# An image laid out as channel and pixel-row pair on 96 partitions, its channel sums in two products, and the third fold moved

## The chip, the core and the metric

The kernel runs on one core of one Trainium2 chip. The metric is device time in microseconds: the median of several executions of the whole kernel.

A core has TensorE (PE), which multiplies matrices into PSUM banks; VectorE (DVE), ScalarE (ACT) and GpSimd (POOL) for elementwise work; and SyncE (SP), which here issues most DMAs. Each engine works through its own queue in order, and engines wait for each other by semaphores.

## What is computed

Inputs are 64 images of 12 channels of 224 x 224 pixels, and 32 text tokens of 192 numbers for each. Three parts follow on each other:

```python
# tokens: 16 x 16 pixels summed, then a weighted sum of the channels
pooled = x.reshape(B, 12, 14, 16, 14, 16).sum(axis=(3, 5))
h = einsum('bcij,ce->bije', pooled, channel_weights).reshape(B, 196, 192)
h = concatenate([h, txt], axis=1)                    # 228 tokens an image
# attention: 12 heads of 16, rotary, causal, with a sink column
h = h + attn(layernorm(h))
# a mixture of 8 experts, top 2, each with a capacity
h = h + moe(layernorm(h))
```

The change touches the first two lines alone, and the time at which some of their work is done.

## The kernel before

**Two passes.** The first pass runs over the 64 images, the second over the 8 experts with tiles of 456 rows. The second is not touched.

**The first pass is a pipeline of five stages.** In each step, image p is pooled (`p`), p-1 gets its queries, keys and values (`a`), p-2 its score maxima (`m`), p-3 its softmax and attention (`t`), and p-4 its projection, routing and scatter (`z`). There are 68 steps; the first six and the last four are written out, the others are a loop over two steps each. Within a step each engine has an order written by hand: `step_tensor` (L1048), `step_scalar` (L1100), `step_vector` (L1144), `pass1_gpsimd` (L1234) and `pass1_sync` (L1210). A stage in brackets below names the batch on which an item works.

**The way of an image.** `load_image` (L404) brings it in one DMA, on 112 partitions: 4 channels x 14 patch rows x 2 halves of a patch row. The free dimension holds three groups (`g`, 4 channels each) of 8 pixel rows x 224. There are two buffers (`xin`), and a load waits until the image two before is pooled (`x_pooled`); SP comes to it one step ahead, so that it is issued as soon as that pooling ends. Then, for each group:

1. `fold_image` (L682, POOL) adds the second 4 pixel rows onto the first 4: one instruction (L686) of 896 elements a partition.
2. `pool_image` (L497, DVE) sums 4 rows x 16 pixels: one reduction (L502) of 896 elements to 14.
3. `spread_patches` (L689, POOL) multiplies the 14 sums with a mask `patch` into 196 columns (L694), so that a partition has its sums only at its own patch row.

`sum_channels` (L837, PE) then makes, for each of two halves of the 196 tokens, three matmuls (L844) that add over the 112 partitions of each group with the channel weights `chan`. Each fp32 matmul is two records in the trace. `copy_h` (ACT) takes the sums out of bank 6.

**The order around the change.** On TensorE the end of a step is T0 T1 T2 (a, L906), `turn_shift` (m, L939), `make_v` (a, L871), `turn_y` (t, L995), T3 T4 T5 (a), `sum_channels` (p, L844), `turn_yn` (t, L1003); the score products S (`score_t`) and C (`score`) open the next step. `turn_shift` waits for `shift_made` and for `routed`; `turn_yn` for `y_normed`.

On DVE it is the maxima 3 to 6 with two pool_images and two `rotate`s (L533, L535) between, pool_image 2, maxima 7 and 8 (L571), `make_shift` (m, L578), `assign` (z, L664 to L679, of which L675 signals `routed`), place_k 1 (a, L559), `split_shift` (m, L586), `weigh` (z), place_k 3, `normalize` (t, L593 and L598, signals `y_normed`), place_k 5.

`make_shift` takes a maximum of two SBUF tensors:

```python
nc.vector.tensor_tensor(shift[:, :, 0:2 * HEADS]..., top[:, :, :]...,
                        sink_tok[:, :]..., ALU.max).then_inc(shift_made, 1)
```

The operands of nearly all other frequent DVE instructions of the pass lie in PSUM, at least one of the two.

On POOL it is inverse_std (a), fold 0, inverse_std (z), fold 1, add_rotation 0 (a, L719), fold 2, add_rotation 1, low_parts 0 and 1 (a, the remainders, two instructions L726 each, the last of them behind ACT's `high_parts` 1), the three spreads, and four scatters (L1284) of an older batch.

Of the kernel before, what the change touches and what calls it, by code (L numbers as in the profile page):

```python
# [21 lines left out]
GRP = 4  # L22
NG = CH // GRP
XP = GRP * SIDE * 2
XF = HALF * IMG
D = 192
# [22 lines left out]
def constants(tokens):  # L49
# [29 lines left out]
    rows = np.arange(XP)  # L79
# [10 lines left out]
        "patch": ((rows[:, None] // 2) % SIDE == np.arange(SIDE)[None]).astype(f),  # L90
# [5 lines left out]
               "before", "patch", "filler"]  # L96
# [28 lines left out]
def build(nc, x, txt, chan_w, norm_scale, norm_bias, w_attn, b_attn, w_proj, b_proj, sinks,  # L125
# [17 lines left out]
    with ctx:  # L143
# [23 lines left out]
        patch = sb("patch", [XP, SIDE])  # L167
        filler = sb("filler", [TT, 2, 2, RW], u32)
        chan = sb("chan", [XP, NG, D])
# [12 lines left out]

        arena = sb("arena", [128, 2 * NG * XF])
        xin = [arena[0:XP, NG * XF * i:NG * XF * (i + 1)].rearrange("p (g f) -> p g f", g=NG) for i in range(2)]
        pooled = [sb(f"pooled{i}", [XP, NG, SIDE]) for i in range(2)]
        spread = sb("spread", [XP, NG, SIDE * SIDE])
# [68 lines left out]
        def view(parts, a, b):  # L255
            nonlocal taken
            taken += a * b
            assert taken <= 2 * NG * XF
            return arena[0:parts, taken - a * b:taken].rearrange("p (a b) -> p a b", a=a)
# [41 lines left out]
        x_spread = sem("x_spread")  # L301
# [52 lines left out]
        N_SMALL = 25  # L354


        def setup_sync(sp):
            for dst, src in (
                (cos[:, :, :], const["cos"]), (sin[:, :, :], const["sin"]), (ident[:, :], const["ident"]),
                (split[:, :], const["split"]), (small[:, :], const["small"]),  # L360
                (patch[:, :], const["patch"]), (filler[:, :, :, :], const["filler"]),
                (scale_col[:, :], norm_scale.rearrange("(c p) -> p c", p=C)),
                (bias_col[:, :], norm_bias.rearrange("(c p) -> p c", p=C)),
                (w_qkv[0:C, :, :], w_attn.rearrange("(c p) n -> p c n", p=C)),
                (b_row, b_attn.rearrange("(a n) -> a n", a=1)),
                (rez[:, :], rezero.rearrange("(a n) -> a n", a=1).to_broadcast([C1, 1])),
                (sink_tok[:, :], sinks.rearrange("(a n) -> a n", a=1).to_broadcast([TT, HEADS])),
                (gate[:, :, :], gate_t.rearrange("(c p) n -> p c n", p=C)),
            ):
# [30 lines left out]
        x_img = x.rearrange("b (g c) (q r) w -> b (c q) g (r w)", g=NG, r=HALF)  # L400
# [281 lines left out]
        def fold_image(pool, at, g):  # L682

            pool.wait_ge(x_loaded[at.par], 16 * (at.half + 1))
            mid = XF // 2
            nc.gpsimd.tensor_tensor(xin[at.par][:, g, 0:mid], xin[at.par][:, g, 0:mid], xin[at.par][:, g, mid:XF],  # L686
                                    ALU.add).then_inc(x_folded, 1)

        def spread_patches(pool, at):  # L689

            wait(pool, h_summed, at.b)
            for g in range(NG):
                pool.wait_ge(x_pooled, NG * at.b + g + 1)
                ins = nc.gpsimd.tensor_tensor(spread[:, g, :].rearrange("p (i j) -> p i j", j=SIDE),  # L694
                                              pooled[at.par][:, g, :].unsqueeze(1).to_broadcast([XP, SIDE, SIDE]),
                                              patch[:, :].unsqueeze(2).to_broadcast([XP, SIDE, SIDE]), ALU.mult)
            ins.then_inc(x_spread, 1)
# [139 lines left out]
        def sum_channels(pe, at):  # L837

            n = at.b + 1
            pe.wait_ge(x_spread, n)  # L840
            wait(pe, v_ready, at.b)
            for t, (lo, hi) in enumerate(((0, TT), (TT, SIDE * SIDE))):
                for g in range(NG):
                    ins = nc.tensor.matmul(bank[6][0:hi - lo, D * t:D * (t + 1)], spread[:, g, lo:hi], chan[:, g, :],  # L844
                                           start=(g == 0), stop=(g == NG - 1))
# [298 lines left out]
        def step_vector(dve, p, a, m, t, z):  # L1144
# [25 lines left out]
            if p:  # L1170
                pool_image(dve, p, 2)
# [5 lines left out]
            if a:  # L1177
                place_k(dve, a, 1)
            if m:
# [54 lines left out]
        def pass1_gpsimd(pool):  # L1234
            def one(half, par, known=None, fill=None):
# [12 lines left out]
                if p:  # L1248
                    fold_image(pool, p, 2)
                if a:  # L1250
# [3 lines left out]
                if p:  # L1254
                    spread_patches(pool, p)
# [446 lines left out]
```

## Time and profile before

| | |
|---|---|
| median of 3 runs | 2946.89 us (2943.04 to 2951.11) |
| the profiled execution | 2948.84 us, of which the span in the trace is 2947.0 |
| PE, matmuls | 2785.7 us busy, 95% of the span |
| DVE | 2049.3 us, 70% |
| POOL | 2023.1 us, 69% |
| ACT | 1693.0 us, 57% |
| first pass | to about 1740 us |

A row of a timeline reads: start in us, duration in us, engine, line of the kernel, operation, output <- inputs, then output and input shapes (partitions x elements; for a matmul stationary rows * columns first), the number of merged records, and in brackets the engine's idle time before it and who ended it. Busy shares are averages; what a change is worth is read from what is late at the place it touches.

### The profile page before, as it was taken

The numbers are of one execution on the slowest core, as the hardware profiler recorded it, in microseconds if no ns is written. First come the engines' busy times: TensorE is split into PE (matmuls) and PEld (weight loads), VectorE is DVE, ScalarE is ACT, GpSimd is POOL, SyncE is SP. The second block draws the span as 40 slices with busy tenths as digits, with TensorE's granted clock in tenths as the row PEclk, the third lists the DMA queues.
The fourth block names the chain that finished last, engine by engine and source line by source line (L and its number), as shares of the span: only waits on it lengthen the run. The fifth ranks groups of instructions, "written<-read, shape, count | busy, mean of one in ns | idle before, by whom it ended". The sixth has DMA issues, their size and how long they took to land. (4 is left out here: it accounts for less than half of the span.)

```text
span 2947.0 us, 65980 instructions
## 1 busy us (share of the span) xinstructions
PE 2785.7 (95%) x21712; PEld 2512.3 (85%) x21712; DVE 2049.3 (70%) x5657; ACT 1693.0 (57%) x4074; POOL 2023.1 (69%) x2070
## 2 busy tenths in 40 slices
PE   2899999999999999999999976999999999999998
PEld 0788888888888888888888865999999989998997
DVE  3477777777777777777777745777676767676766
ACT  0365666666666666656666644656565656555655
POOL 2478888888888888888888833666555656565665
PEclk9899999999999999999999987999999999999999
DMA  6444555543444444334444113333333333323242
GB/s 177 145 163 162 172 177 182 160 117 106 109 116 121 121 121 117 110 104 115 121 121 121 54 43 68 50 60 56 63 50 61 56 61 54 66 45 66 44 70 43
DMA packets 206006, 292.47 MB, mean 99 GB/s; under 512 B 95670, under 2 KB 167675, under 8 KB 205874
## 3 DMA queue, kind: packets, MB, share of 16 engines
q1 hardware_dynamic: 82994, 243.82, 28.3%
q0 software_dynamic: 122880, 47.00, 11.3%
q8 instruction: 69, 1.13, 0.2%
q14 instruction: 63, 0.52, 0.1%
HBM read 201.73 MB, written 93.90 MB: 100 GB/s over the span
## 5 line engine op out<-in xcount | busy, mean ns | idle before, releaser
L1493 POOL DMA_INDIRECT out<-arena,who x320 | 596.0, 1862 | 292.1 <-DVE who L1372 179.7
L686 POOL TENSOR_TENSOR arena<-arena 112x896 f32<-112x896 f32 x192 | 403.0, 2100 | 44.0 <-DMA arena<-in_x 44.0
L571 DVE TENSOR_REDUCE top<-bank 114x2 f32<-114x456 f32 (+1 forms) x576 | 352.7, 622 | 87.3 <-PE bank L930 71.1
L1466 PE MATMUL bank<-w_dn,hid 128*114 128x192 f32 x3840 | 401.9, 264 | 0.0
L1466 PEld LDWEIGHTS bank<-w_dn,hid 128*114 128x114 f32 x3840 | 390.3, 180 | 0.0
L1439 ACT ACTIVATE arena<-bank 128x456 f32<-128x456 f32 x320 | 176.3, 551 | 341.8 <-PE bank L1430 331.8
L1284 POOL DMA_INDIRECT moe_rows<-row,slot x256 | 294.5, 1150 | 77.3 <-issue 73.7
L548 ACT ACTIVATE pieces<-bank 64x456 fp32r<-64x456 f32 x384 | 209.4, 545 | 147.1 <-PE bank L906 144.8
L1443 DVE TENSOR_TENSOR arena<-bank,arena 128x456 f32<-128x456 f32 x320 | 201.5, 630 | 94.9 <-ACT arena L1439 82.4
L726 POOL TENSOR_TENSOR qk<-rot_c,qk 114x384 fp32r<-114x384 f32 x256 | 253.9, 1014 | 18.3 <-ACT qk L747 18.3
L1426 PE MATMUL bank<-pieces 128*128 128x456 f32 x640 | 240.2, 375 | 22.5 <-DVE arena L1443 15.5
L805 ACT ACTIVATE prob<-bank 115x456 f32<-115x456 f32 x384 | 208.0, 542 | 80.7 <-PE bank L956 80.0
L1455 DVE TENSOR_TENSOR hid<-arena,hid 128x456 fp32r<-128x456 f32 x320 | 201.6, 630 | 52.3 <-ACT hid L1450 34.3
L1430 PE MATMUL bank<-pieces 128*128 128x456 f32 x640 | 237.8, 372 | 0.0
L1450 ACT ACTIVATE hid<-arena 128x456 fp32r<-128x456 f32 x320 | 187.0, 584 | 87.9 <-DVE arena L1443 86.7
L1429 PE MATMUL bank<-pieces 128*128 128x456 f32 x640 | 237.1, 371 | 0.0
L1427 PE MATMUL bank<-pieces 128*128 128x456 f32 x640 | 236.2, 369 | 0.6 <-issue 0.4
L1428 PE MATMUL bank<-pieces 128*128 128x456 f32 x640 | 236.7, 370 | 0.0
L502 DVE TENSOR_REDUCE pooled<-arena 112x14 f32<-112x896 f32 x192 | 206.7, 1076 | 26.4 <-POOL arena L686 26.4
L1483 POOL TENSOR_TENSOR rms<-rms,minus_half 114x4 f32<-114x4 f32 x82 | 85.4, 1041 | 190.3 <-DVE rms L1364 190.3
L906 PE MATMUL bank<-ident_r,qk 114*128 114x114 f32 x1536 | 202.1, 282 | 10.6 <-POOL qk L726 10.6
L906 PEld LDWEIGHTS bank<-ident_r,qk 114*128 114x128 f32 x1536 | 186.5, 196 | 23.0 <-POOL qk L726 22.9
(171 smaller groups left out, 7211.4 us busy)
## 6 DMA issues: line engine op xcount, KB each, us to landing
arena<-in_x SPq DMA_DIRECT2D x64, 2352.0 KB, 11.9
arena<-moe_rows SPq DMA_DIRECT2D x82, 363.4 KB
moe_rows<-filler SPq DMA_DIRECT2D x20, 1453.5 KB
out<-h SPq DMA_DIRECT2D x64, 171.0 KB
out<-arena,who POOLq DMA_INDIRECT x320, 5.0
arena<-in_w_t SPq DMA_DIRECT2D x9, 512.0 KB, 6.8
arena<-in_w_t SPq DMA_DIRECT2D x18, 256.0 KB, 7.7
moe_rows<-row,slot POOLq DMA_INDIRECT x256, 7.1
```

The source lines that it names most:

```text
L571: nc.vector.tensor_reduce(dst, src, AX.X, ALU.max).then_inc(maxed[k], 1)
L686: nc.gpsimd.tensor_tensor(xin[at.par][:, g, 0:mid], xin[at.par][:, g, 0:mid], xin[at.par][:, g, mid:XF], ALU.add).then_inc(x_folded, 1)
L726: ins = nc.gpsimd.tensor_tensor(lo, of, first.bitcast(fp32), ALU.subtract)
L906: ins = nc.tensor.matmul(dst[:, TT * (2 * pair + half):TT * (2 * pair + half + 1)], src, ident_r[0:TT, 0:TT], start=True, stop=True)
L1284: nc.gpsimd.indirect_dma_start(out=moe_rows[0:SLOTS, :], out_offset=bass.IndirectOffsetOnAxis(ap=slot[at.par][:, 2 * t + k:2 * t + k + 1], ...
L1426: nc.tensor.matmul(dst, hi[:, 0, col], za_hi[:, :], start=True, stop=False)
L1427: nc.tensor.matmul(dst, hi[:, 0, col], za_lo[:, :], start=False, stop=False)
L1428: nc.tensor.matmul(dst, lo[:, 0, col], za_hi[:, :], start=False, stop=False)
L1429: nc.tensor.matmul(dst, hi[:, 1, col], zb[:, :], start=False, stop=False)
L1430: ins = nc.tensor.matmul(dst, lo[:, 1, col], zb[:, :], start=False, stop=True)
L1466: ins = nc.tensor.matmul(dst, hid2[:, j, h_part, at], w_dn2[e_par][:, j, w_part, :], start=(j == 0 and s % 2 == 0 and part == 0), stop=(j ...
L1493: nc.gpsimd.indirect_dma_start(out=out[:, :], out_offset=bass.IndirectOffsetOnAxis(ap=who[par][:, s:s + 1], axis=0), in_=ys[par][:, s, :], ...
```

## The change

**Layout.** A partition now holds one of 12 channels and one of 8 pairs of pixel rows within a patch row: 12 x 8 = 96 partitions. The free dimension is 14 patch rows of 2 x 224 pixels. An image comes by 8 DMAs, one for each pair of pixel rows, 12 partitions each.

**Folds and pools.** A fold adds the second pixel row of each pair onto the first, and a pool sums 16 pixels. They are done in three bands of patch rows, 5, 5 and 4 of the 14, where three groups of channels were.

**Channel sums.** A partition now has all 196 patch sums of its channel and row pair, so `pooled` goes straight into the matmul, with the channel weights repeated for the 8 row pairs: two matmuls instead of six. `spread_patches`, its mask and its semaphore are gone; `sum_channels` waits for `x_pooled`.

**Order.** On POOL fold 2 moves from behind add_rotation 0 to behind low_parts 1, where the spreads were. On DVE pool_image 2 moves from before maxima 7 and 8 to behind place_k 1, before split_shift.

```diff
-GRP = 4
-NG = CH // GRP
-XP = GRP * SIDE * 2
-XF = HALF * IMG
+XP = CH * HALF
+XF = 2 * IMG
+BANDS = ((0, 5), (5, 10), (10, SIDE))
+NG = len(BANDS)
...
-        chan = sb("chan", [XP, NG, D])
+        chan = sb("chan", [XP, D])
...
-        arena = sb("arena", [128, 2 * NG * XF])
-        pooled = [sb(f"pooled{i}", [XP, NG, SIDE]) for i in range(2)]
-        spread = sb("spread", [XP, NG, SIDE * SIDE])
+        arena = sb("arena", [128, 2 * SIDE * XF])
+        pooled = [sb(f"pooled{i}", [XP, SIDE * SIDE]) for i in range(2)]
...
-            for g in range(NG):
-                sp.dma_start(chan[:, g, :], chan_w[GRP * g:GRP * (g + 1), :].unsqueeze(1)
-                             .to_broadcast([GRP, SIDE * 2, D])).then_inc(loaded, 16)
+            sp.dma_start(chan[:, :], chan_w.unsqueeze(0).to_broadcast([HALF, CH, D])).then_inc(loaded, 16)
...
-        x_img = x.rearrange("b (g c) (q r) w -> b (c q) g (r w)", g=NG, r=HALF)
+        x_img = x.rearrange("b c (i r s) w -> b r c i (s w)", r=HALF, s=2)
...
-            sp.dma_start(xin[at.par][:, :, :], x_img[at.b, :, :, :]).then_inc(x_loaded[at.par], 16)
+            for r in range(HALF):
+                sp.dma_start(xin[at.par][CH * r:CH * (r + 1), :, :], x_img[at.b, r, :, :, :]).then_inc(x_loaded[at.par], 16)
...
             if g == 0:
-                wait(dve, x_spread, at.b - 1)
+                wait(dve, h_summed, at.b - 1)
             dve.wait_ge(x_folded, NG * at.b + g + 1)
+            lo, hi = BANDS[g]
             ins = nc.vector.tensor_reduce(
-                pooled[at.par][:, g, :],
-                xin[at.par][:, g, 0:XF // 2].rearrange("p (r j c) -> p j r c", r=HALF // 2, c=PATCH), AX.XY, ALU.add)
+                pooled[at.par][:, SIDE * lo:SIDE * hi],
+                xin[at.par][:, lo:hi, 0:IMG].rearrange("p i (j c) -> p i j c", c=PATCH), AX.X, ALU.add)
...
-            pool.wait_ge(x_loaded[at.par], 16 * (at.half + 1))
-            mid = XF // 2
-            nc.gpsimd.tensor_tensor(xin[at.par][:, g, 0:mid], xin[at.par][:, g, 0:mid], xin[at.par][:, g, mid:XF],
+            pool.wait_ge(x_loaded[at.par], 16 * HALF * (at.half + 1))
+            lo, hi = BANDS[g]
+            nc.gpsimd.tensor_tensor(xin[at.par][:, lo:hi, 0:IMG], xin[at.par][:, lo:hi, 0:IMG], xin[at.par][:, lo:hi, IMG:XF],
                                     ALU.add).then_inc(x_folded, 1)
-
-        def spread_patches(pool, at):
...
-            pe.wait_ge(x_spread, n)
+            pe.wait_ge(x_pooled, NG * n)
...
-                for g in range(NG):
-                    ins = nc.tensor.matmul(bank[6][0:hi - lo, D * t:D * (t + 1)], spread[:, g, lo:hi], chan[:, g, :],
-                                           start=(g == 0), stop=(g == NG - 1))
+                ins = nc.tensor.matmul(bank[6][0:hi - lo, D * t:D * (t + 1)], pooled[at.par][:, lo:hi], chan[:, :],
+                                       start=True, stop=True)
...
             maxima("6")
-            if p:
-                pool_image(dve, p, 2)
             maxima("7 8")
...
                 place_k(dve, a, 1)
+            if p:
+                pool_image(dve, p, 2)
             if m:
                 split_shift(dve, m)
...
                     add_rotation(pool, a, 0)
-                if p:
-                    fold_image(pool, p, 2)
-                if a:
                     add_rotation(pool, a, 1)
                     low_parts(pool, a, 0)
                     low_parts(pool, a, 1)
                 if p:
-                    spread_patches(pool, p)
+                    fold_image(pool, p, 2)
```

## Rows read from the trace of the kernel before

**Rows 1.** Busy by stretch: start:end, length, PE, PEld, DVE, ACT, POOL, clock, DMA, GB/s

```profile
800.00:1200.00 400.00, 396.10 (x3411) 349.35 (x3409) 298.38 (x907) 245.28 (x546) 326.82 (x405) 1.00 0.42 115
...
1710.00:1736.00 26.00, 21.33 (x203) 19.39 (x202) 16.30 (x66) 13.42 (x29) 10.18 (x12) 0.98 0.14 37
```

**Rows 2.** Timeline of TensorE, the end of one step and its next

```profile
1013.44 0.27 PE L930 MATMUL bank<-mask_q,ident_r 114*114 114x228 f32 x1
...
1014.50 1.55 PE L906 MATMUL bank<-ident_r,qk 114*128 114x114 f32 x12
1016.00 0.39 PE L939 MATMUL bank<-ident,shift 114*128 114x114 f32 x2
1016.23 1.47 PE L871 MATMUL bank<-w_qkv,xn_t 97*114 97x192 f32 x8
...
1018.10 1.53 PE L906 MATMUL bank<-ident_r,qk 114*128 114x114 f32 x12
1019.47 2.16 PE L844 MATMUL bank<-chan,spread 112*114 112x192 f32 x12
1021.47 0.56 PE L1003 MATMUL bank<-ident,yn 114*97 114x114 f32 x4
...
1040.06 1.55 PE L906 MATMUL bank<-ident_r,qk 114*128 114x114 f32 x12
1041.93 0.39 PE L939 MATMUL bank<-ident,shift 114*128 114x114 f32 x2 [0.33 <-DVE slot L675]
```

**Rows 3.** Timeline of DVE in the same step

```profile
1004.68 0.56 DVE L533 TENSOR_TENSOR rot_c<-bank,cos 114x384 f32<-114x384 f32 x1 [1.54 <-PE bank L862]
...
1012.52 1.07 DVE L502 TENSOR_REDUCE pooled<-arena 112x14 f32<-112x896 f32 x1
1013.51 1.16 DVE L571 TENSOR_REDUCE top<-bank 114x2 f32<-114x456 f32 x2
1014.71 0.21 DVE L578 TENSOR_TENSOR shift<-top,sink_tok 114x48 f32<-114x48 f32 x1
...
1017.40 0.45 DVE L586 SCALAR_TENSOR_TENSOR shift_t<-shift_hi,split,bank 128x228 fp32r<-128x228 f32 x1 [0.92 <-ACT shift_hi L795]
...
1020.43 0.42 DVE L598 TENSOR_TENSOR yn<-bank,rden 114x96 f32<-114x96 f32 x2
```

**Rows 4.** Timeline of POOL in the same step, and a first fold later

```profile
1012.31 1.99 POOL L726 TENSOR_TENSOR qk<-rot_c,qk 114x384 fp32r<-114x384 f32 x2 [0.27 <-ACT qk L747]
1014.25 1.53 POOL L694 TENSOR_TENSOR spread<-pooled,patch 112x196 f32<-112x196 f32 x3
...
1050.97 2.10 POOL L686 TENSOR_TENSOR arena<-arena 112x896 f32<-112x896 f32 x1
```

**Rows 5.** All of L578 (min/median/max ns); timelines around it in two other steps

```profile
L578 DVE TENSOR_TENSOR shift<-top,sink_tok x64: 207/588/614, 106.8 to 1731.7; 114x48 f32<-114x48 f32 x64
...
106.19 1.00 POOL L726 TENSOR_TENSOR qk<-rot_c,qk 114x384 fp32r<-114x384 f32 x1
106.80 0.45 DVE L578 TENSOR_TENSOR shift<-top,sink_tok 114x48 f32<-114x48 f32 x1
...
1039.77 1.01 POOL L694 TENSOR_TENSOR spread<-pooled,patch 112x196 f32<-112x196 f32 x2
1040.24 0.60 DVE L578 TENSOR_TENSOR shift<-top,sink_tok 114x48 f32<-114x48 f32 x1
1041.62 0.16 DVE L675 SCALAR_TENSOR_TENSOR slot<-bank,slot_f 114x4 uint32<-114x4 f32 x1
```

**Rows 6.** Timeline of TensorE in step 64, the first without an image

```profile
1716.11 0.63 PE L1003 MATMUL bank<-ident,yn 114*97 114x114 f32 x4 [1.30 <-DVE yn L598]
```

**Rows 7.** The image's DMAs: all 64 landings, and one issue on SP

```profile
DMA to landing us min/median/max: 10.9/11.9/23.6
...
1013.77 0.32 SPq L406 DMA_DIRECT2D arena<-in_x  x1
```

**Rows 8.** Timeline of TensorE in step 1

```profile
84.85 4.14 PE L844 MATMUL bank<-chan,spread 112*114 112x192 f32 x12
```

More of the change, by code:

```diff
@@ L78, in constants @@
             filler[:, par, s, COL_ID] = tokens + (par * T + 2 * q + s) % ROWS
-    rows = np.arange(XP)
     return {
@@ L89, in constants @@
         "before": (q[:, None] < q[None, :]).astype(f),
-        "patch": ((rows[:, None] // 2) % SIDE == np.arange(SIDE)[None]).astype(f),
         "filler": filler,
@@ L95 @@
 CONST_NAMES = ["cos", "sin", "ident", "mask_q0", "mask_k", "sel", "split", "small",
-               "before", "patch", "filler"]
+               "before", "filler"]
 class Batch:
@@ L166, in build @@
         ones = sb("ones", [TT, TT], bf16)
-        patch = sb("patch", [XP, SIDE])
         filler = sb("filler", [TT, 2, 2, RW], u32)
-        chan = sb("chan", [XP, NG, D])
+        chan = sb("chan", [XP, D])
         scale_col = sb("scale_col", [C, 2])
@@ L179, in build @@
         gate = sb("gate", [C, 2, E])
-        arena = sb("arena", [128, 2 * NG * XF])
-        xin = [arena[0:XP, NG * XF * i:NG * XF * (i + 1)].rearrange("p (g f) -> p g f", g=NG) for i in range(2)]
-        pooled = [sb(f"pooled{i}", [XP, NG, SIDE]) for i in range(2)]
-        spread = sb("spread", [XP, NG, SIDE * SIDE])
+        arena = sb("arena", [128, 2 * SIDE * XF])
+        xin = [arena[0:XP, SIDE * XF * i:SIDE * XF * (i + 1)].rearrange("p (i f) -> p i f", i=SIDE) for i in range(2)]
+        pooled = [sb(f"pooled{i}", [XP, SIDE * SIDE]) for i in range(2)]
         h = [sb(f"h{i}", [TT, 2, D]) for i in range(2)]
@@ L257, in view @@
             taken += a * b
-            assert taken <= 2 * NG * XF
+            assert taken <= 2 * SIDE * XF
             return arena[0:parts, taken - a * b:taken].rearrange("p (a b) -> p a b", a=a)
@@ L300, in build @@
         x_pooled = sem("x_pooled")
-        x_spread = sem("x_spread")
         h_summed = sem("h_summed")
@@ L352, in build @@
         added = [sem(f"added{i}") for i in range(2)]
-        N_SMALL = 25
+        N_SMALL = 22
         def setup_sync(sp):
@@ L360, in setup_sync @@
                 (split[:, :], const["split"]), (small[:, :], const["small"]),
-                (patch[:, :], const["patch"]), (filler[:, :, :, :], const["filler"]),
+                (filler[:, :, :, :], const["filler"]),
                 (scale_col[:, :], norm_scale.rearrange("(c p) -> p c", p=C)),
@@ L682, in fold_image @@
         def fold_image(pool, at, g):
-            pool.wait_ge(x_loaded[at.par], 16 * (at.half + 1))
-            mid = XF // 2
-            nc.gpsimd.tensor_tensor(xin[at.par][:, g, 0:mid], xin[at.par][:, g, 0:mid], xin[at.par][:, g, mid:XF],
+            pool.wait_ge(x_loaded[at.par], 16 * HALF * (at.half + 1))
+            lo, hi = BANDS[g]
+            nc.gpsimd.tensor_tensor(xin[at.par][:, lo:hi, 0:IMG], xin[at.par][:, lo:hi, 0:IMG], xin[at.par][:, lo:hi, IMG:XF],
                                     ALU.add).then_inc(x_folded, 1)
-        def spread_patches(pool, at):
-            wait(pool, h_summed, at.b)
-            for g in range(NG):
[L693 to L697, printed above, removed]
         def inverse_std(pool, at, norm):
@@ L839, in sum_channels @@
             n = at.b + 1
-            pe.wait_ge(x_spread, n)
+            pe.wait_ge(x_pooled, NG * n)
             wait(pe, v_ready, at.b)
             for t, (lo, hi) in enumerate(((0, TT), (TT, SIDE * SIDE))):
-                for g in range(NG):
-                    ins = nc.tensor.matmul(bank[6][0:hi - lo, D * t:D * (t + 1)], spread[:, g, lo:hi], chan[:, g, :],
-                                           start=(g == 0), stop=(g == NG - 1))
+                ins = nc.tensor.matmul(bank[6][0:hi - lo, D * t:D * (t + 1)], pooled[at.par][:, lo:hi], chan[:, :],
+                                       start=True, stop=True)
             ins.then_inc(h_summed, 1)
```

## The prediction

> **What bounds the kernel now.** I read the busy times by stretch first. Between 800 and 1200 us, which stands for the whole first pass, TensorE is busy 396.10 of 400 us at granted clock 1.00 [rows 1]. A step (one image in, one batch out) takes (1731.7 - 106.8) / 63 = 25.79 us, from the first and last of 64 starts of L578 [rows 5]. So work taken off TensorE is worth its time only until another engine is late for it. The step timelines of PE, DVE and POOL tell which one. All times below are from 1000 us on, for the step at 1014.
>
> TensorE's order there is T0-T2 at 14.50, turn_shift at 16.00, make_v at 16.23, T3-T5 at 18.10, sum_channels at 19.47, turn_yn at 21.47, and the next T0 at 40.06 [rows 2]. turn_shift needs `shift_made` and, through `routed`, the end of `assign`; turn_yn needs `y_normed`, the last but one item of the DVE step. Both already press: turn_shift of the next step waited 0.33 us for DVE's L675 [rows 2], and DVE's L598 ends at 20.43 + 0.42 = 20.85, 0.6 us before turn_yn starts [rows 3]. Step 64 has no image, hence no sum_channels, and there turn_yn waited 1.30 us for L598 [rows 6]. Taking all 2.0 us away gained 0.7.
>
> **Removed from TensorE.** sum_channels is 12 records from 19.47 to 21.47, 2.00 us for 6 matmuls; 2 remain, 0.67 us, so 1.33 us go. Contraction over 96 instead of 112 partitions changes nothing: L871, over 97, takes 1.47 us for 8 records where L844 takes 2.16 for 12; with the last record's tail of 0.16 taken off either, 0.164 each against 0.167 [rows 2]. The end of sum_channels moves from 21.47 to 20.14.
>
> **Removed from POOL.** Three spreads, 1.53 us at 14.25 [rows 4], and the wait of sum_channels for them. Nothing waited for POOL there but sum_channels, which started 3.7 us later.
>
> **Folds and pools made larger.** The two first bands have 5 x 224 = 1120 elements instead of 896, the third 4 x 224 = 896. A fold of 896 takes 2.10 us [rows 4], so one of 1120 at most 2.10 x 1.25 = 2.63, +0.5 each; a pool of 1.07 us [rows 3] gets at most +0.27. DVE stood idle 1.54 us before rotate 0 [rows 3], and the norm1 chain in front of POOL starts earlier with sum_channels, so I cost these at 0 (bounds 0 to +0.3 a step, should fold 1 make DVE's second pool late).
>
> **Fold 2 behind the remainders.** This is the decisive edit. low_parts, two in all of 1.99 us at 12.31, end at 14.25, where the first spread started [rows 4]. They were waiting for ScalarE's high parts, so the earlier removal of fold 2 from the queue does not bring them forward. Fold 2 now runs from 14.25 to 14.25 + 2.10 = 16.35.
>
> DVE meanwhile reaches make_shift, L578. Its last score (C8) leaves TensorE at 13.44 + 0.27 = 13.71 [rows 2]; the last two maxima take 1.16 us [rows 3], so L578 comes at 14.6, and in no case before 13.71 + 0.58 = 14.3. pool_image 2 no longer stands before it, but it had been hidden in the wait for these scores, so this brings it 0.1 us. L578 is the one frequent DVE instruction here with two SBUF tensor inputs, and its rows show what a running POOL instruction does to it. It takes 207 ns at best and 588 in the median [rows 5]. At 1014.71 it came between two spreads and took 0.21. At 1040.24 it came as the second of two spreads (1039.77, 1.01 together) had begun, and ended at 40.84, 0.06 behind that spread. At 106.80 it came in the middle of a low_parts that ended at 107.19, and ended at 107.25, again 0.06 behind, though the remainder here was another instruction of another length. So it isn't slowed by a share; it is held until the POOL instruction is through, and gets in before the next [rows 3, 5]. In front of a fold begun at 14.25 it is held to 16.35 and ends at 16.41, not 14.92 or, in the slow kind, 15.3.
>
> No row of before shows a hold behind an instruction of 2.1 us. The Trainium skill, SBUF — State Buffer, section "SBUF: two separate sides", says that a two-SBUF-input Vector instruction and a GpSimd instruction take an exclusive lock on the shared ports for the whole instruction. By that rule the hold is the rest of the fold, as I take it; were the hold capped at the 0.4 us that rows show, the sum would be that of rival B. The rule speaks against this change.
>
> What follows, step by step. From the end of L578 to the end of L675 are 41.78 - 40.84 = 0.94 us [rows 5]; `routed` is at 16.41 + 0.94 = 17.35. TensorE took 0.15 from L675's end to turn_shift (41.78 to 41.93) [rows 2, 5]: it starts at 17.50 instead of 16.00, stall 1.50. Behind it in TensorE's queue make_v, turn_y, T3-T5 and sum_channels take 19.47 - 16.00 = 3.47, to 20.97, and sum_channels 0.67, to 21.64. On DVE, end of L578 to end of L598 were 20.85 - 14.92 = 5.93 us, of which 0.92 idle ahead of L586, waiting for ScalarE [rows 3]. The idle is gone, and pool_image 2 (0.99 from its start at 12.52 to the next at 13.51) is in its place: 5.93 - 0.92 + 0.99 = 6.00, so L598 ends at 22.41 and turn_yn starts at about 22.50, a second stall of 0.86. From turn_yn to the next T0 is 40.06 - 21.47 = 18.59 [rows 2]. The new step is 22.50 - 14.50 + 18.59 = 26.59 us, against 25.79: **+0.80 us**. About 60 steps (4 to 63) have it: +48.
>
> **The load.** It is now 8 DMAs, with 1344 runs of 1792 bytes where there were 336 of 7168. SP spends 0.32 on an issue [rows 7], 2.6 us for eight; queued behind it is store_h2, which waits for the next step's residual anyway. Landing took 11.9 us in the median, and the image issued at 13.77 is not the next to be folded but the one after it, at 50.97 [rows 4, 7], 37 us later. Even three times the time would be in time; cost 0 in the loop, also with the issue behind a later pool_image 2. At the start it is open: the longest landing was 23.6. I take +4 us for the first image (0 to +10), +1 for its folds, -0.5 for spreads.
> The Trainium skill, DMA: Bandwidth & Descriptors, section on why a DMA increments its semaphore by 16, says that a transfer uses the largest number of DMA engines up to 16 that divides its slowest dimension. By that an image on 12 partitions per DMA runs on 12 engines, an estimate of 16/12 x 11.9 = 16 us, still hidden; no row here can show it.
>
> **Ramp.** In steps 0 to 2 TensorE ran at its lower level, and sum_channels took 4.14 us [rows 8]; two thirds of it are 2.76 at most, three times, and 1.3 in step 3: -9.6 at most, of which I take -8.5. With +4.5 that is -4. Sum: +48 - 4 = +44 on the profiled execution's 2948.84 (span 2947.0), 0.07% above the median of 2946.89. **Forecast 2991 us.**
>
> **Rivals.**
> A, the forecast: held behind the fold. Its own range is 0.6 to 1.05 us a step, and ramp -10 to +10: 2973 to 3018. Chance 0.66.
> B, the other side: L578 isn't held longer than it is now. Then L598 still ends at 20.85, because pool_image 2 fits in the 0.92 idle [rows 3]; turn_yn starts at about 20.95 instead of 21.47, -0.52, and the 0.33 in every other step goes, -0.21. 60 x 0.73 = 44, ramp 4: 2899. It decides at fold 2's start: if L578 reaches the port first. For it: two instructions of 0.52 and 0.99 are all that rows show. Against it: three arrivals with one law, and a margin of 0.4 us between 14.25 and 14.6. Chance 0.19.
> C, in every other step the one and the other, as L578's two kinds alternate now: 60 x (0.80 - 0.73) / 2 = +2, ramp -4: 2945. Chance 0.07.
> D, all of TensorE's gain arrives: 60 x 1.33 = 80, ramp 4: 2863. Step 64 speaks against it [rows 6]. Chance 0.03.
> E, slower still: stalls of 2.4 in 26.6 us lower the clock, or the image is late. At 21.33 busy of 26 us the clock was still 0.98 [rows 1]. Above 3018. Chance 0.05.
>
> **How the numbers follow.** A measurement of this kernel tells 0.3%, about 9 us, from no change. Slower by more: A and E, 0.71. Faster: B and D, 0.22, and a part of C, together 0.23. Within: 0.06. A alone holds less than 8 in 10, so the range has to reach to B: 2893 to 3018; the likeliest case's own range is 2973 to 3018.
>
> **What would show it.** L578 with a mean near 1.9 us, its records ending 0.06 behind fold 2; PE idle about 1.5 before L939 with DVE's L675 as releaser, and about 0.9 before turn_yn with L598; sum_channels at 4 records in 0.67; PE's busy share in the loop near 91%; no idle of POOL for the image but in the first steps. It would be wrong if L578 stays at 0.6, if low_parts end later than the maxima (then L578 slips in before the fold), or if POOL waits for the image.

## The result and the profile after

The changed kernel takes 3378.24 us in the median of 5 runs (3368.72 to 3406.98), beside 2947.48 of 5 runs of the kernel before (2943.04 to 2955.78) on the same chip: ratio 1.1466, 95% interval 1.1429 to 1.1503. The forecast was 2991, in 2893 to 3018. The sign was right and the size wrong by a factor of nearly ten: +431 us where +44 was forecast. The profiled execution, the slowest of the five, has a span of 3405.2 us, +458.2 on the 2947.0 of before.

The page of the changed kernel: the granted clock and the DMA share in 40 slices, and two of its costliest groups.

```profile
span 3405.2 us, 65814 instructions
...
PEclk9887877788789898888989888879999999999999
DMA  6677767777667677666777775033324333243332
...
L681 POOL TENSOR_TENSOR arena<-arena 96x1120 f32<-96x1120 f32 (+1 forms) x192 | 462.4, 2409 | 54.8 <-DMA arena<-in_x 54.8
...
L510 DVE BATCH_NORM_STATS2 st<-h 114x6 f32<-114x192 f32 x256 | 79.5, 352 | 263.4 <-DMA h<-in_txt 204.8
```

In 21 of the 26 slices of the first pass the clock is below 90%; on the page of before it is in one. The DMA engines are 60 to 80% busy in nearly all of them. VectorE waited 204.8 us for the text tokens. Busy by stretch, as in [rows 1] (start:end, length, PE, PEld, DVE, ACT, POOL, clock, DMA share, GB/s):

```profile
400.00:800.00 400.00, 311.27 (x2214) 265.14 (x2213) 218.33 (x601) 165.76 (x364) 211.34 (x240) 0.80 0.71 114
800.00:1200.00 400.00, 362.95 (x2675) 316.31 (x2674) 271.17 (x741) 206.02 (x448) 259.67 (x294) 0.85 0.69 102
```

Between 800 and 1200 TensorE was busy 396.10 us at clock 1.00 with a DMA share of 0.42; now it is 362.95 at 0.85 with 0.69. There were 115 GB/s and are 102: more busy DMA engines move less.

The starts of make_shift give the steps. In the 20 steps from the third on, in which SP also fills the expert slots, a step takes (972.8 - 215.8) / 20 = 37.9 us. In the 40 behind them it takes 29.9 in the mean, and the single steps are of four kinds: 26.7, 28, 30.5 and 33.5.

Now the decisive place, in a later step in which nothing waits for a DMA. TensorE, VectorE and GpSimd in answer to [rows 2 to 4]:

```profile
1511.51 0.61 PE L923 MATMUL bank<-ident,shift 114*128 114x114 f32 x2 [1.42 <-DVE slot L670]
1511.92 2.77 PE L855 MATMUL bank<-w_qkv,xn_t 97*114 97x192 f32 x8
...
1516.61 0.86 PE L828 MATMUL bank<-chan,pooled 96*114 96x192 f32 x4
1517.80 0.44 PE L987 MATMUL bank<-ident,yn 114*97 114x114 f32 x2 [0.33 <-DVE yn L593]
```

```profile
1507.47 1.17 DVE L566 TENSOR_REDUCE top<-bank 114x2 f32<-114x456 f32 x2 [0.84 <-PE bank L914]
1508.67 1.75 DVE L573 TENSOR_TENSOR shift<-top,sink_tok 114x48 f32<-114x48 f32 x1
...
1511.20 0.16 DVE L670 SCALAR_TENSOR_TENSOR slot<-bank,slot_f 114x4 uint32<-114x4 f32 x1
```

```profile
1508.26 2.11 POOL L681 TENSOR_TENSOR arena<-arena 96x896 f32<-96x896 f32 x1
```

make_shift (L573 here) takes 1.75 us and ends at 1510.42, 0.05 behind fold 2. turn_shift (L923) waits 1.42 us for the slots, turn_yn (L987) 0.33. sum_channels is 4 records. All of that is the forecast's mechanism. But make_v (L855), straight behind the wait, takes 2.77 us for its 8 records, where it took 1.47: half speed. That also makes the second wait look short: the slower make_v brings TensorE later to turn_yn. One of the steps of 26.7 us shows the two waits without it (granted clock 1.00 from 1631.7 to 1658.3):

```profile
1631.90 1.47 PE L855 MATMUL bank<-w_qkv,xn_t 97*114 97x192 f32 x8
...
1636.72 0.63 PE L987 MATMUL bank<-ident,yn 114*97 114x114 f32 x4 [0.72 <-DVE yn L593]
```

turn_shift waited 1.43 there, and turn_yn 0.72. The source view of make_shift counts the waits (durations min/median/max, first and last start; then who waited for it, in us and times):

```profile
L573 DVE TENSOR_TENSOR shift<-top,sink_tok x64: 209/1750/2095, 138.1 to 2190.9; 114x48 f32<-114x48 f32 x64
...
  PEld bank L923: 93.6, 62
```

62 waits of 1.5 us are 94 us. They don't make 458.

### The profile page after: what moved, and what is told of

It is laid out like the page before. It is cut to its first block and busy times, and to the rows that moved or that the text cites. A ratio compares the mean times of both kernels' runs of the same rounds, so it can differ in the third digit from the quotient of the medians.

```text
span 3405.2 us, 65814 instructions
## 1 busy us (share of the span) xinstructions
PE 2982.1 (88%) x21200; PEld 2666.4 (78%) x21200; DVE 2172.5 (64%) x5657; ACT 1710.9 (50%) x4074; POOL 1983.0 (58%) x1878
## 5 line engine op out<-in xcount | busy, mean ns | idle before, releaser
L681 POOL TENSOR_TENSOR arena<-arena 96x1120 f32<-96x1120 f32 (+1 forms) x192 | 462.4, 2409 | 54.8 <-DMA arena<-in_x 54.8
L690 POOL TENSOR_TENSOR var<-mv,ln_eps 114x2 f32<-114x2 f32 x128 | 24.9, 195 | 550.4 <-DVE mv L514 550.4
L711 POOL TENSOR_TENSOR qk<-rot_c,qk 114x384 fp32r<-114x384 f32 x256 | 253.5, 1011 | 44.5 <-ACT qk L732 44.5
L497 DVE TENSOR_REDUCE pooled<-arena 96x70 f32<-96x1120 f32 (+1 forms) x192 | 235.9, 1228 | 60.5 <-POOL arena L681 60.5
L704 POOL TENSOR_TENSOR rot_c<-rot_c,rot_s 114x192 f32<-114x192 f32 x256 | 145.3, 587 | 175.7 <-DVE rot_s L530 175.7
L510 DVE BATCH_NORM_STATS2 st<-h 114x6 f32<-114x192 f32 x256 | 79.5, 352 | 263.4 <-DMA h<-in_txt 204.8
L890 PE MATMUL bank<-ident_r,qk 114*128 114x114 f32 x1536 | 237.5, 313 | 10.1 <-POOL qk L711 10.0
L890 PEld LDWEIGHTS bank<-ident_r,qk 114*128 114x128 f32 x1536 | 221.9, 227 | 22.4 <-POOL qk L711 22.2
```

The lines of the kernel that those rows point to most:

```text
L681: nc.gpsimd.tensor_tensor(xin[at.par][:, lo:hi, 0:IMG], xin[at.par][:, lo:hi, 0:IMG], xin[at.par][:, lo:hi, IMG:XF], ALU.add).then_inc(x_f ...
L711: ins = nc.gpsimd.tensor_tensor(lo, of, first.bitcast(fp32), ALU.subtract)
L890: ins = nc.tensor.matmul(dst[:, TT * (2 * pair + half):TT * (2 * pair + half + 1)], src, ident_r[0:TT, 0:TT], start=True, stop=True)
```

## The experiments

The kernel before ran beside each. "Slot steps" are the mean of the 20 steps in which slots are filled, "later" that of the 40 after; both and the clock are of the profiled run.

| kernel | median us | ratio (95%) | slot steps | later | clock |
|---|---|---|---|---|---|
| before | 2947 | | 25.8 | 25.8 | 0.98 |
| changed | 3378 | 1.147 (1.143 to 1.150) | 37.9 | 29.9 | 0.89 |
| e1_spread | 3159 | 1.071 (1.067 to 1.076) | 29.6 | 29.2 | 0.91 |
| e6_sink_psum | 2969 | 1.004 (1.002 to 1.007) | 27.4 | 25.6 | 0.98 |
| e11_sink_only | 3488 | 1.183 (1.181 to 1.185) | 37.6 | 31.7 | 0.90 |
| e5_order | 3445 | 1.166 (1.162 to 1.170) | 37.7 | 30.7 | 0.90 |
| e4_spread_order | 2951 | (see there) | 27.3 | 25.1 | 0.98 |
| e7_stall | 3125 | 1.057 (1.053 to 1.061) | 28.8 | 28.7 | 0.93 |
| e8_text_act | 2930 | 0.993 (0.990 to 0.995) | 26.0 | 25.1 | 0.97 |
| e9_text_only | 3337 | 1.129 (1.126 to 1.132) | 36.1 | 29.0 | 0.90 |
| e10_patch_rows | 3227 | 1.093 (1.088 to 1.098) | 30.3 | 30.6 | 0.90 |
| e2_short_runs (of before) | 2948 | 0.999 (0.998 to 1.000) | 25.7 | 25.7 | 0.98 |
| e3_crowd (of before) | 3448 | 1.169 (1.165 to 1.173) | 30.4 | 35.3 | 0.91 |

**e1_spread: the same eight DMAs, their 12 partitions 8 apart.**

```
-sp.dma_start(chan[:, :], chan_w.unsqueeze(0).to_broadcast([HALF, CH, D]))...
+sp.dma_start(chan[:, :], chan_w.unsqueeze(1).to_broadcast([CH, HALF, D]))...
...
-    sp.dma_start(xin[at.par][CH * r:CH * (r + 1), :, :], x_img[at.b, r, :, :, :])...
+    sp.dma_start(xin[at.par][r:XP:HALF, :, :], x_img[at.b, r, :, :, :])...
```

> The changed kernel with one thing altered: a partition is channel x 8 + row pair instead of row pair x 12 + channel. Still 8 DMAs an image, 12 partitions each, 1792-byte runs; but the 12 partitions of a DMA now lie 8 apart instead of side by side (the channel weights are repeated to match). Theory P (the load is slow because each of its DMAs writes 12 adjacent partitions): the load about doubles its rate, the text no longer comes late, and the first 20 steps fall from 38.5 us to the 30 of the later ones or less; total 3100 to 3200. Theory R (it is slow because of its short runs) and theory N (because it is eight DMAs on few DMA engines): nothing moves, 3378. In all of them L573 stays held for 1.75 us, by the forecast's theory of the hold.

It takes 3158.84, 219 less in median and 239.8 in span, and its eight issues still last 7.57 us. Nothing else differs: not the runs of 1792 bytes, not the 12 partitions a DMA, not the number of DMAs. What cost was that the partitions were adjacent. Stretches of 3 us inside one image's load, columns as above: the changed kernel, e1_spread, and the kernel before.

```profile
1521.00:1524.00 3.00, 3.00 (x28) 2.88 (x27) 2.41 (x8) 2.07 (x5) 2.92 (x3) 1.00 0.82 110
1524.00:1527.00 3.00, 3.00 (x29) 2.01 (x28) 1.70 (x3) 1.92 (x4) 2.84 (x4) 1.00 0.80 108
```

```profile
1521.00:1524.00 3.00, 3.00 (x14) 2.78 (x14) 1.51 (x5) 1.61 (x4) 0.00 (x0) 0.50 0.81 161
1524.00:1527.00 3.00, 3.00 (x22) 2.92 (x22) 1.47 (x5) 1.46 (x4) 2.25 (x5) 0.95 0.79 177
```

```profile
1533.00:1536.00 3.00, 3.00 (x26) 2.99 (x25) 2.76 (x14) 2.35 (x5) 2.39 (x3) 1.00 1.00 265
```

At the same busy share of about 0.8 the changed load moves 108 to 110 GB/s here and the spread one 161 and 177; over all stretches of these two loads with a share of 0.77 or more it is 108 to 135 and 151 to 209. An image of 2.41 MB takes 2.41 / 0.109 = 22 us at the changed kernel's rate, and 2.41 / 0.265 = 9 at that of before. The Trainium skill, SBUF — State Buffer, section "Door 1: The DMA port swizzle", says that a DMA's bandwidth depends on how many of 16 ports its partitions reach, and that four adjacent partitions share one: 12 adjacent ones reach 3, the spread ones 8. The order of the rates agrees. Its 436 GB/s over 16 ports would give 82 for three and 218 for eight, both estimates; the traces show 108 to 135, more than that, and 151 to 209.

The middle fence also shows the second matter: the granted clock is 0.50 in its first row, that is 1.2 GHz, as in the two stretches ahead of it (1515 to 1521): 9 us, right behind TensorE's wait of 1.42 us at 1514.33.

**e2_short_runs and e3_crowd: the two properties, each alone, on the kernel before.** The first cuts the image into four DMAs along the free dimension (all 112 partitions, runs of 1792 bytes), the second into seven of 16 adjacent partitions (runs of 7168 bytes).

```
 e2_short_runs
-            sp.dma_start(xin[at.par][:, :, :], x_img[at.b, :, :, :])...
+            for r in range(4):
+                sp.dma_start(xin[at.par][:, :, 448 * r:448 * (r + 1)], x_img[at.b, :, :, 448 * r:448 * (r + 1)])...
 e3_crowd
-            sp.dma_start(xin[at.par][:, :, :], x_img[at.b, :, :, :])...
+            for r in range(7):
+                sp.dma_start(xin[at.par][16 * r:16 * (r + 1), :, :], x_img[at.b, 16 * r:16 * (r + 1), :, :])...
```

> The kernel before with its image cut into 4 DMAs, each with 2 of the 8 pixel rows of every group, on all 112 partitions: 1344 runs of 1792 bytes as in the changed kernel, nothing else altered. Theory R: each image costs as much DMA time as in the changed kernel (DMA share 0.7 instead of 0.42 between 800 and 1200 us), text late in the first 20 steps, total above 3150. Theory P: the load stays about as it was, 2947 to 2960. Theory N (few DMA engines): 2947 to 2960 too.

> The kernel before with its image cut into 7 DMAs of 16 adjacent partitions each: the runs stay 7168 bytes, 336 of them, nothing else altered. Theory P: the image takes clearly longer than 12 us, 22 us or more, SP stands in its issue, and the first 20 steps get longer; total 3000 to 3250. Theory R and a theory that blames only the number of DMA engines: as before, 2947 to 2960.

Queue rows (packets, MB, share of 16 engines' span) of before, e2_short_runs and e3_crowd:

```profile
q1 hardware_dynamic: 82994, 243.82, 28.3%
```

```profile
q1 hardware_dynamic: 150578, 243.83, 29.7%
```

```profile
q1 hardware_dynamic: 89138, 243.84, 43.4%
```

Short runs, in four DMAs, cost nothing in the time of the kernel. Seven DMAs to adjacent partitions, without any part of the change, cost 17%: 43.4% of 3439.8 against 28.3% of 2947.0 is 1.8 times the packet time for the same bytes. A stretch of e3_crowd's load, and in its timeline what came late behind it:

```profile
1515.00:1518.00 3.00, 3.00 (x32) 2.75 (x34) 2.55 (x7) 2.53 (x6) 2.84 (x4) 1.00 0.95 123
```

```profile
1525.21 0.98 ACT L772 ACTIVATE row<-h,shifted,rstd 114x192 f32<-114x192 f32 x2 [6.92 <-DMA moe_rows<-row,slot]
```

The image itself is in time. ScalarE waits for the scatters of an earlier batch, whose row buffer it must refill; in the median they land 16.8 us after issue where it was 7.1. That they are late because the image's packets are under way is the likely reading; no row shows it directly. In the changed kernel itself the scatters are not late: 6.3 us.

**e6_sink_psum: e1_spread without the hold.** One operand of make_shift moves to PSUM, and nothing is reordered.

```
+        sink_top = bank[7][0:TT, 2 * T:2 * T + HEADS]
...
-            nc.vector.tensor_scalar(sink_tok[:, :], sink_tok[:, :], 4.0, None, ALU.mult)
+            nc.vector.tensor_scalar(sink_top, sink_tok[:, :], 4.0, None, ALU.mult)
...
-                                    sink_tok[:, :].unsqueeze(1).unsqueeze(1).to_broadcast([TT, 2, 2, HEADS]),
+                                    sink_top.unsqueeze(1).unsqueeze(1).to_broadcast([TT, 2, 2, HEADS]),
```

> e1_spread with one operand moved: L573 reads the sink row from PSUM instead of SBUF, so it has one SBUF tensor input. Fold 2 stays behind the remainders and runs beside it as before. Theory H (two SBUF inputs are held for a running POOL instruction, and the waits that this makes let TensorE's clock fall): L573 takes 0.21 to 0.3 us with fold 2 running, turn_shift does not wait, the clock is 0.97 or more between 800 and 1200 us, the step is 25.0 to 25.3 us, total 2900 to 2960. Theory F (the order itself, fold 2 and pool_image 2 late, makes the steps long): the step stays above 27 us although L573 is short, total above 3050.

A stretch of the loop in e1_spread and in e6_sink_psum, and the source view of make_shift in the latter:

```profile
800.00:1200.00 400.00, 376.76 (x2909) 330.50 (x2909) 292.45 (x799) 221.54 (x484) 283.02 (x317) 0.89 0.46 100
```

```profile
800.00:1200.00 400.00, 386.16 (x3304) 334.44 (x3303) 304.92 (x898) 248.28 (x544) 317.76 (x360) 0.99 0.53 116
```

```profile
L574 DVE TENSOR_TENSOR shift<-top,bank x64: 203/204/206, 105.2 to 1756.6; 114x48 f32<-114x48 f32 x64
```

With fold 2 still running over it, make_shift takes 204 ns every time. So the hold hangs on its two SBUF inputs, and with it go 197.4 us of span and the low clock. The exclusive lock of the Trainium skill, SBUF — State Buffer, section "SBUF: two separate sides", which the forecast set against rival B, is borne out for a whole instruction of 2.11 us. TensorE still waits 0.86 us for `normalize` in each later step of e6_sink_psum, and its clock between 800 and 1200 us is 0.99 all the same.

**e4_spread_order and e7_stall: is it the hold, or the wait of TensorE?** The first is e1_spread with fold 2 and pool_image 2 back at their old places; the second adds an idle reduction of about 1.6 us on VectorE in front of make_shift, so that TensorE waits as in the changed kernel, but with no hold at all.

```
 e4_spread_order, on e1_spread
                     add_rotation(pool, a, 0)
+                if p:
+                    fold_image(pool, p, 2)
...
+            if p:
+                pool_image(dve, p, 2)
             maxima("7 8")
 e7_stall, on e4_spread_order
+            nc.vector.tensor_reduce(idle[:, :], sel[:, :, :].bitcast(fp32), AX.X, ALU.max)
             dve.wait_ge(maxed[8], n)
```

> The changed kernel with the spread partitions of e1_spread and with fold 2 and pool_image 2 at their old places (behind add_rotation 0; before maxima 7 and 8). Theory H (hold): L573 is at 0.21 us again, turn_shift no longer waits for L670, turn_yn waits about 0.1 to 0.8 us for the normalize, the step is 25.0 to 25.3 us, and the clock stays at 1.00 because the waits of 1.4 us are gone: 2880 to 2915. If the clock dips come from something else in the new layout (fewer matmuls), they stay: 3000 or more.

> e4_spread_order with an idle reduction over a constant (one SBUF input, about 1.6 us) put on DVE directly before L573: it makes turn_shift late by about 1.5 us with no hold, no layout and no order of the changed kernel's POOL queue. Theory H's second half (a wait of TensorE of 1.4 us in each step at this place is what lets the clock fall, whatever makes it): the clock falls to 0.85 to 0.93 in the loop, steps of 26.7, 28 and 30.5 us come in turn as in e1_spread, total 3100 to 3200. If the wait alone counts, without the clock: steps of 25.1 + 0.9 to 1.5, total 3000 to 3040 at clock 1.00.

The same stretch in the one and the other, and one of e7_stall's waits:

```profile
800.00:1200.00 400.00, 390.79 (x3373) 338.54 (x3371) 305.98 (x928) 254.00 (x559) 325.21 (x366) 1.00 0.53 119
```

```profile
800.00:1200.00 400.00, 376.60 (x2977) 328.82 (x2977) 297.70 (x839) 228.15 (x497) 288.77 (x326) 0.92 0.48 106
```

```profile
1027.61 0.61 PE L925 MATMUL bank<-ident,shift 114*128 114x114 f32 x2 [1.30 <-DVE slot L672]
1028.02 2.77 PE L857 MATMUL bank<-w_qkv,xn_t 97*114 97x192 f32 x8
```

A later step grows from 25.1 to 28.7 us. The shortest are 26.1, so the wait itself costs 1.0; the other 2.6 come from the steps in which TensorE runs part of the time at 1.2 instead of 2.4 GHz, and the slow part begins with this wait: make_v behind it takes 2.77 again. The three runs e1_spread, e6_sink_psum and e7_stall settle it: a wait of 1.3 to 1.4 us at this place, in each step, takes the clock down, be it made by the hold or by the idle reduction.

e4_spread_order ran in 2950.87, 2951.6 and 2952.64 us, and once in 2907.15, beside 2948.36 for the kernel before; the profiled run is the first, of the long kind. I didn't find what the 44 us were, and take no verdict from it. Its steps are what counts here: 25.1 in the loop, and in the slot steps some of 30 to 33, in which the text was late (VectorE waited 36.6 us for it, 11 times).

**e8_text_act and e9_text_only: the text.** The text is issued by ScalarE instead of SP, once on e4_spread_order and once on the changed kernel.

```
 sync:
-                if p:
-                    load_text(sp, p)
...
 step_scalar:
             exps("5")
+            if p:
+                load_text(act, p)
```

> e4_spread_order with the text's DMA issued by ScalarE (behind the exponential 5) instead of SyncE, so that it stands neither behind the image's issues nor in the same DMA queue. Theory T (in the first 20 steps, while slots are filled, the long steps of 30 to 33 us come from the text arriving late behind the image): no wait of L510 for the text in the loop, the first 20 steps are 25 to 25.5 us like the others, total 2890 to 2910 in every run. Otherwise (the image or the fill is late itself): long steps stay, 2905 to 2955 as e4.

> The changed kernel with that one alteration: the text's DMA on ScalarE's queue, the slow load and everything else left. Theory T: of the 12.7 us by which the first 20 steps are longer than before, most goes, and they become like the later ones, 29 to 31 us unless the image is late in its turn; total about 3180 to 3250. If the load's own rate bounds these steps (image 20 us and fill in one queue), POOL now waits for the image instead and the total stays above 3300.

The timeline of a slot step of the changed kernel shows why the text was suspected:

```profile
519.44 16.53 SPq L405 DMA_DIRECT2D h<-in_txt  x1
536.23 0.29 SPq L409 DMA_DIRECT2D moe_rows<-filler  x1
536.77 20.70 SPq L400 DMA_DIRECT2D arena<-in_x  x8
...
548.02 0.62 DVE L510 BATCH_NORM_STATS2 st<-h 114x6 f32<-114x192 f32 x2 [12.81 <-DMA h<-in_txt]
...
549.71 0.70 PE L903 MATMUL bank<-mask_q,ident_r 114*114 114x456 f32 x1 [9.99 <-DVE top L566]
```

Eight issues last 20.70 us, the issue of the text 16.53, and TensorE stands for 9.99 in the end. On the fast load, e8_text_act is the best kernel of the study, 0.75% under the one before. On the slow load the text out of the way gains little, 37.9 to 36.1 us a slot step, since the next in line takes its place (waits from 200 to 700 us: total, times, longest):

```profile
POOL arena L681 <- DMA arena<-in_x: 85.3, 13, 8.0
```

So what bounds the slot steps is the load, and the text was only the first to be late behind it. My guess had been that the text alone was late.

**e5_order: the slow load with both moves undone.** It is the changed kernel with the order edit of e4_spread_order.

> The changed kernel with its slow load left as it is (12 adjacent partitions a DMA) and only the two moves undone: fold 2 behind add_rotation 0, pool_image 2 before maxima 7 and 8. With e1_spread and e4_spread_order it completes the square of load and hold. Theory: L573 is at 0.21 us and the clock in the loop rises from 0.85; the load, about 24 us at 108 GB/s behind 8 issues, still bounds the first 20 steps at 36 us or more; in the later steps it may just fit under 25.1 us. Later steps 25.1 to 27.5 us instead of 29.9, total 3150 to 3270. If the slow load is what lets the clock fall, the later steps stay near 30 and the total near 3378.

A miss: 3445, slower than the changed kernel, though make_shift is at 209 ns in the median and TensorE no longer waits there. Later steps are 30.7 us, nearly all alike. The timeline of one:

```profile
1525.60 8.41 SPq L400 DMA_DIRECT2D arena<-in_x  x8
...
1533.33 0.49 ACT L774 ACTIVATE val<-bank 114x384 f32<-114x384 f32 x1 [2.58 <-remote]
1533.49 0.63 DVE L554 CAST pieces<-bank 128x456 fp32r<-128x456 f32 x1 [1.73 <-remote]
...
1533.96 0.88 PE L828 MATMUL bank<-chan,pooled 96*114 96x192 f32 x4 [2.23 <-ACT val L774]
```

ScalarE and VectorE both stand with an input that TensorE had given more than 1.5 us earlier (make_v, for ScalarE's copy_v, ended at 1529.5, and the last of T3 to T5 at 1531.7), and go on in the 0.7 us before the end of SP's issues at 1534.0. The profile names no releaser ("remote").

**e10_patch_rows: e8_text_act with the image in 14 DMAs, each to all 96 partitions.**

```
-        x_img = x.rearrange("b c (i r s) w -> b r c i (s w)", r=HALF, s=2)
+        x_img = x.rearrange("b c (i r s) w -> b i c r (s w)", r=HALF, s=2)
...
-            for r in range(HALF):
-                sp.dma_start(xin[at.par][r:XP:HALF, :, :], x_img[at.b, r, :, :, :])...
+            for i in range(SIDE):
+                sp.dma_start(xin[at.par][:, i, :], x_img[at.b, i, :, :, :])...
```

> e8_text_act with the image cut by patch row instead of by row pair: 14 DMAs an image, each over all 96 partitions with one run of 1792 bytes a partition. Theory P says that what counts is how many different partitions are written at a time; here each of the DMA engines in use still walks through the partitions of one channel, as in e8, so the rate in the loop should be that of e1_spread, 150 to 200 GB/s, not that of the changed kernel, although the cut is another: later steps 25.1 us, total 2905 to 2950. If a DMA's cost goes by the number of issues, 14 of them make SP late and the total is above 2960.

A miss as well. The load is light (24.9% of the engines' span, less than the 28.3% of before), yet the kernel takes 3227. Its timeline:

```profile
1530.38 14.56 SPq L400 DMA_DIRECT2D arena<-in_x  x14
...
1538.08 0.49 ACT L774 ACTIVATE val<-bank 114x384 f32<-114x384 f32 x1 [1.46 <-remote]
...
1538.72 1.60 PE L828 MATMUL bank<-chan,pooled 96*114 96x192 f32 x4 [2.20 <-ACT val L774]
```

So this stall doesn't need a slow load. It came while SP's issues lay over copy_v (L774), but that alone doesn't make it: in the steps between 1200 and 1500 us of e4_spread_order and e8_text_act a train of eight issues lies over copy_v too, from 4.6 us before its start to 3 us after, and there is no such wait. Here SP's train went on to 1544.9 while the engines resumed at 1538. Neither the end of SP's issues nor the load's rate explains both. **This cause is open.** What is shown is that a lighter load, bought with more issues, can cost more than it saves.

**e11_sink_only: the slow load without the hold.** It is the edit of e6_sink_psum on the changed kernel, and completes the square of the two causes.

> The changed kernel with one edit: make_shift reads its sink operand from PSUM, as in e6_sink_psum. The slow load (12 adjacent partitions a DMA) and the changed order stay. With e1_spread and e6_sink_psum this completes a square of load and hold. Both theories: make_shift takes about 0.2 us instead of 1.75, and the steps in which slots are filled stay near 38 us, since there the load's own rate sets the pace. Theory L (outside those steps the load costs little, and the hold with the clock that it lowers is the rest): later steps near 25.6 us, as in e6_sink_psum; the time is that of e6_sink_psum, 2969, plus 20 steps of 38.5 less 27.8, 214: about 3185, in 3150 to 3230. Theory S (the stall of ScalarE and VectorE while SyncE issues the image, seen in e5_order, comes with the slow load whenever TensorE is not held up elsewhere): later steps near 30 us with waits of copy_v of 2 us, the time 3185 + 41 x 4.5, about 3370.

3488, beyond both theories. The stall of e5_order isn't there; it is that of e3_crowd:

```profile
1286.63 1.19 POOL L1266 DMA_INDIRECT moe_rows<-row,slot  x1 [0.20 <-issue]
...
1305.56 0.98 ACT L756 ACTIVATE row<-h,shifted,rstd 114x192 f32<-114x192 f32 x2 [7.20 <-DMA moe_rows<-row,slot]
...
1306.59 0.99 PE L1006 MATMUL bank<-ident,row 114*96 114x114 f32 x4 [5.76 <-ACT row L756]
```

An image is issued at 1287.72, 1.1 us behind the first of four scatters (the last at 1290.96), and ScalarE gets its row buffer only at 1305.56. Later steps go from 25.5 to 37.7 us, by where the load falls.

The square, in spans of the profiled runs: with both, 3405.2 (the changed kernel); load alone 3481.5; hold alone 3165.4; neither 2968.0. The slow load costs 513.5 without the hold and 239.8 with it; the hold costs 197.4 on the fast load and on the slow one gains 76.3. In medians (3378.2, 3488.1, 3158.8, 2969.4) the same four differences are 519, 219, 189 and 110. They are not to be added: either alone is far beyond the forecast, and on the slow load the hold's longer wait takes the place of waits for scatters. With the hold the image is issued later: in the changed kernel 2.6 us behind the first scatter (1510.55 and 1513.16), when two of the four are out, and here 1.1. Whether that is why its scatters aren't late, no run shows.

## Why the prediction was wrong

**What held.** The forecast's values stand in brackets. Fold 2 takes 2.11 us (2.10), make_shift ends 0.05 behind it (0.06), turn_shift waits 1.42 (1.50), and sum_channels is 4 records. In the steps at full clock turn_yn waits 0.72 (0.86) and a step takes 26.67 (26.59): as long as the clock holds, the sum of A is right term by term, not by luck. But only 4 of the 40 later steps are of this kind. That make_shift is held was the right choice between A and B.

B's case, the moves without the hold, is e6_sink_psum. turn_yn waits 0.86 there, and B had it at 20.95 - 20.14 = 0.81. Its undisturbed steps are 25.3 and 25.5 in turn; B's sum says 25.79 - 0.73 = 25.06. Two slips in the working change nothing: A's own range comes to 3020 by its terms, not 3018, and half of the 0.33 that B takes away is 0.17, not 0.21.

**Failed: "cost 0 in the loop"** for the load. The step weighed one thing, whether this image is there in time for its fold, and gave it 37 us. That was nearly right: GpSimd waits for an image only once, 54.8 us for the first. It left out who shares the DMA engines. At 109 GB/s an image keeps them busy for 22 of the 26 us of a step, and in the slot steps the filler comes on top. What is late is then the text (160 us of VectorE's waits in the slot steps) and SP's own queue; where the hold is taken away, in e11_sink_only, it is the scatters. In place of the +4 for the load the runs show +239.8 us in the changed kernel, by e1_spread: 50 before the third step, 757 - 592 = 165 in the slot steps, the rest in the others. The thing to ask was in the diff, the destination of each DMA: 12 adjacent partitions where there were 112; the landing of 11.9 us in [rows 7] holds only for the latter. The estimate of 16 us by the number of engines looked at another property, one that e1_spread has too.

**Failed: the clock, left to rival E.** Forecast A priced the waits at their length, which gave +0.80 a step over before. The steps that keep the clock bear that out (26.67 - 25.79 = 0.88), but 36 of 40 don't keep it, and the mean is 29.9. On the fast load, without the load's part in it, the wait itself costs 1.0 (e7_stall) to 1.1 us (e1_spread, 26.7 against 25.6) and the clock that it takes down 2.5 to 2.6 more (29.2 - 26.7, 28.7 - 26.1). In all, e1_spread less e6_sink_psum is 197.4 us, by an estimate some 60 x 1.1 = 66 of it the wait and the other 131 the clock. The argument against was one stretch with 21.33 of 26 us busy at 0.98 [rows 1], a stretch behind the loop, once. That a stretch kept its clock once says little of a wait that comes back 60 times; the weight of E, 0.05, was far too low, and the range ended below it. Of E's two conditions it was the stalls that came true; GpSimd waited for no image but the first.

**Mis-sized: SP's issues,** 0.32 each by [rows 7]. Eight to 12 partitions each last 7.56 us in the later steps, 0.95 each, and up to 20.70 in the slot steps. Under the fast load this is hidden in the later steps (25.1 in e4_spread_order). In the slot steps it may have a part in the late text, but there e8_text_act against e4_spread_order is 21 us in medians, so it isn't what made the time.

**The rest,** folds, pools, ramp: e6_sink_psum is the whole change without the slow load and without the hold, and stands 21.0 us of span above before. Its slot steps, 27.4 on average, are the cost: the text is late in 13 of them, by 44.5 us in all. Its later steps, 25.6, are the gain, smaller than B's. Three of the 40 take 27 to 29 us (clock 0.88 in the one that starts at 1095.5), and in the others pool_image 2, which B fitted into an idle time of 0.92, takes 1.08; from make_shift's end to `normalize`'s it is 6.22 us (1018.38 to 1024.60), where B kept 5.93. In e4_spread_order, where pool_image 2 stands at its old place, turn_yn waits less. Its waits from 1000 to 1500 us in e6_sink_psum and e4_spread_order (total, times, longest):

```profile
PE bank L988 <- DVE yn L594: 16.3, 19, 0.9
```

```profile
PE bank L987 <- DVE yn L593: 10.6, 20, 0.6
```

Against these +21 the forecast had +1 for the folds, -0.5 for the spreads and -8.5 for the ramp, and nothing for the text behind the image's issues. e8_text_act, with both moves undone and the text off SP, is 25 us faster than before, of the 44 that B promised for the loop.

## What to carry to other kernels

When a load is cut along partitions, look at which partitions each piece writes: in the stretches of 3 us inside a load, 12 adjacent ones gave 108 to 135 GB/s and 16 adjacent ones 122 to 148, where 12 spread ones gave 151 to 209 and all 112 at once 239 to 304. The first to suffer were the small transfers behind it, not its own reader. Price a wait of TensorE that comes back in each step by the clock as well as by its length: here 1.3 to 1.4 us cost 3.6 a step. Before an instruction with two SBUF inputs is let run beside a long one on GpSimd, move one operand to PSUM: on the fast load that alone was worth 197 us. On the slow load the same edit cost 76 (110 in medians), so mend the load first.

## What the runs showed of the hardware that I had not expected

- The rate hangs on adjacency: same bytes, runs, DMAs and partitions per DMA, 108 to 110 against 161 and 177 GB/s in the stretches shown. With runs of 1792 instead of 7168 bytes the time is 0.999 (0.998 to 1.000) of that before.
- An issue on SP isn't a fixed price: 0.32 us for an image to 112 partitions, 0.95 for one to 12 in the later steps, and in a slot step 2.6 for one to 12 and 16.5 for the text.
- While SP issued 8 or 14 DMAs, ScalarE stood before copy_v with its input there, 2.0 us in the mean in 40 steps of e5_order and 1.6 in 49 of e10_patch_rows, and VectorE before place_k 1.3 and 0.9. It came in these two of the thirteen kernels alone. The mechanism is open.
- A recurring wait of 1.3 to 1.4 us in a stream that is otherwise full took the granted clock between 800 and 1200 us from 1.00 to 0.89 and 0.92 (e1_spread, e7_stall). One of 0.86 us in each step left it at 0.99 (e6_sink_psum).
